# Relative attention on one core: scores that wait by pairs of heads, and three steps moved within a sequence's four quads

## The chip, the cores and the metric

The kernel runs on 1 core of one Trainium2 chip. The metric is the time of one execution in device microseconds (us), as the median of the runs shown. The program is a decoder of six stages in a row; the change touches one of them, the relative attention, and nothing before or behind it.

## What is computed

The stage takes 32 sequences of 100 rows (queries) of width 256 and, for each, a context of 361 rows (keys and values). It is attention with 16 heads of 16 channels, with a learnt vector for the distance between query and key in the scores, and another in the sum:

```python
rq, rk, rv = heads(query @ Wq + bq), heads(key @ Wk + bk), heads(value @ Wv + bv)
attn1 = einsum('bhqd,bhkd->bhqk', rq, rk)
attn2 = einsum('bhqd,qkd->bhqk', rq, rel_k_table[idx])
attn  = softmax((attn1 + attn2) / sqrt(16), axis=-1)
w1 = einsum('bhqk,bhkd->bhqd', attn, rv)
w2 = einsum('bhqk,qkd->bhqd', attn, rel_v_table[idx])
x = (w1 + w2).transpose(0, 2, 1, 3).reshape(b, t, 256) @ Wo + bo
```

`idx` is the distance from query to key, cut off at -32 and 32, plus 32. The stage's result is then x = layernorm(x + this). All of it is in 32-bit floats.

## The kernel before

**One turn per sequence, four quads in a turn.** `relative_cross` (L1827) runs a loop of turns, one for each of the 32 sequences, with each engine's instructions written out in a fixed order. The 16 heads go in four quads (`g` = 0 to 3) of four heads. The scores of a quad have the four banks of `rel_ps_s` in PSUM, one per head, and there is one set of them: a quad's scores may be written only when the weights of the quad before have been read out.

**A quad on three engines.** On TensorE, `scores` (L2334) computes four heads, each on 32 rows of the array of its own; the semaphore `s_s` is raised after the second and after the fourth. On VectorE, `maxima` (L2226) takes the heads in two pairs: it adds the distances' part (`rel_r_key`, L2235) and takes the negated maximum of each row (L2238). On ScalarE, `weights` (L2126) takes the exponentials of a pair (L2136), two instructions of one head each, and after the second pair raises `s_p`. Then ScalarE sends the quad's weights to DRAM (`store`, L2148).

**The transposes are one quad behind.** `weightsT` on TensorE transposes the weights of the quad before in three steps (c = 0, 1, 2, L2356) into the one bank `rel_ps_t`; after each, ScalarE copies it away (L2124) before the next may be written. `sums` on TensorE multiplies the values with the transposed weights of two quads before (`rel_ps_o`). So in quad g ScalarE's order is: copy 0, exponentials of pair 0, copy 1, exponentials of pair 1, copy 2.

**The jobs.** All else that TensorE does goes through the two banks of `rel_ps_m`, as 14 jobs per turn in the order of the table `JOBS`; a job's bank is its number modulo 2, and it may begin only when the job two before it, in the same bank, has been emptied by VectorE or ScalarE. `PLACES` has 16 places, four in each quad (place 4g behind the scores, 4g+1, 4g+2 and 4g+3 behind the transposes 0, 1 and 2), and says which jobs stand there. The jobs are `xT` and `q` (rows transposed, queries), `r0` and `r1` (the queries against the distance table, for the sequence two ahead), `k0`, `k1`, `v0`, `v1`, `v2` (keys and values of the next sequence), and of the sequence before: `den` (denominators; VectorE inverts them at L2216), `d0` and `d1` (transposes of the weights by distance, L2313), `w2` (sum with the distance table, L2321 and L2325) and `out` (output product).

**The weights by distance.** SyncE reads the stored weights of the sequence before back from DRAM by diagonals into `rel_by_dist`. Its first column, for all keys beyond the cut-off, is the far sum: GpSimd masks the weights (`rel_far`) and VectorE sums them at L2265, when both `rel_far` and the transfer are there. `d0` and `d1` wait for this sum. `den` waits for `rel_raw`, VectorE's copy of the finished sums of the sequence before (L2257), which waits for the last `sums` of that sequence; this stands on TensorE in quad 1, behind `r0`.

The loop of VectorE before, for each quad (L2250 and on): both pairs' maxima, in quad 1 the copy to `rel_raw`, then the jobs that VectorE empties, and at the end of quad 1 the far sum.

Of the kernel before, what the change touches and what calls it, by code (L numbers as in the profile page):

```python
# [12 lines left out]
AX = mybir.AxisListType  # L13
# [1813 lines left out]
def relative_cross(nc, io, keep):  # L1827
# [31 lines left out]
    with ExitStack() as ctx:  # L1859
# [55 lines left out]
        s_rpad = sem("distances_padded")  # L1915
        s_rout, s_rkey = sem("distances_in_dram"), [sem(f"distances_by_key{v}") for v in range(2)]
        s_s, s_add, s_neg, s_p = sem("scores"), sem("scores_added"), sem("maxima_negated"), sem("weights_ready")
        s_t, s_t_sb, s_pv, s_att = sem("weights_transposed"), sem("weightsT_stored"), sem("values_summed"), sem("sums_kept")
        s_pout, s_pdist, s_far, s_far_sum = ([sem(f"weights{v}_in_dram") for v in range(2)], sem("weights_by_distance"), sem("far_masked"),
                                             sem("far_summed"))  # L1920
# [3 lines left out]
        def head_of(g, j):  # L1924
# [2 lines left out]

        AHEAD = {"after": 2, "next": 1, "last": -1}
        JOBS = [("after", "xT"), ("next", "k0"), ("after", "q"), ("next", "k1"), ("after", "r0"), ("next", "v0"),
                ("after", "r1"), ("next", "v1"), ("last", "den"), ("last", "d0"), ("last", "d1"), ("last", "w2"),  # L1930
                ("next", "v2"), ("last", "out")]
        PLACES = [[0], [1], [2], [3], [4], [5], [6], [], [7], [8], [9, 10], [], [11], [12], [13], []]
        NUMBER = {what: n for n, (_, what) in enumerate(JOBS)}

        def bank(what):
# [151 lines left out]
        def _(act):  # L2087
            act.wait_ge(s_ready, 1)
            act.sem_inc(s_p, 1)

            def empty(t, place):
                for n, what, b in jobs(t, place):
# [33 lines left out]
            def weights(t, g, k):  # L2126
                if not t.within(B):
                    return
                act.wait_ge(s_neg, PAIRS * t.i + (2 * g + k + 1))
                if g == 0 and k == 0 and (not isinstance(t.i, int) or t.i > 1):  # L2130

                    act.wait_ge(s_pout[t.parity], 16 * GROUPS * t.half)
                    act.wait_ge(s_far, t.i - 1)
                for j in range(2 * k, 2 * k + 2):
                    slot = QUAD * g + j
                    last = nc.scalar.activation(prob[:, t.parity, slot, :], ps_s[0:S, j, 0:L], ACT.Exp,  # L2136
                                                bias=nmx[:, slot:slot + 1])
                if k == 1:
                    last.then_inc(s_p, 1)

            def store(b, g):
                if not b.within(B):
# [25 lines left out]
        def _(dve):  # L2168
# [79 lines left out]
            def turn(t):  # L2248
# [2 lines left out]
                    normalise(t + 2)  # L2251
                for g in range(GROUPS):
                    maxima(t, g, 0)
                    maxima(t, g, 1)
                    if g == 1 and prev.within(B):
                        dve.wait_ge(s_pv, GROUPS * prev.i + GROUPS)
                        nc.vector.tensor_copy(raw[:], ps_raw).then_inc(s_att, 1)  # L2257
                    for k in range(4):
                        if g == GROUPS - 1 and k == 2:
                            normalise(t + 3)  # L2260
                        empty(t, 4 * g + k)
                    if g == 1 and prev.within(B):
                        dve.wait_ge(s_far, prev.i + 1)
                        dve.wait_ge(s_pdist, 16 * prev.i + 16)
                        nc.vector.reduce_sum(by_dist[:, :, 0], far[:], AX.X).then_inc(s_far_sum, 1)  # L2265

            turns(dve, turn, -2, 3, B - 3, B + 1)

# [1 line left out]
        def _(pe):  # L2270
# [63 lines left out]
            def scores(t, g):  # L2334
                if not t.within(B):
                    return
                pe.wait_ge(s_p, GROUPS * t.i + (g + 1))
                if g == 0:
                    pe.wait_ge(s_qh, t.i + 1)
                    wait_emptied(pe, t + -1, "k1")  # L2340
                for j in range(QUAD):
                    rows = slice(j * TILE, (j + 1) * TILE)
                    last = mm(ps_s[0:S, j, 0:L], q_par[rows, t.parity, g % 2, g // 2, :], kT[rows, t.parity, g // 2, :], 0, 1)
                    if j % 2:
                        last.then_inc(s_s, 1)
# [621 lines left out]
```

## Time and profile before

| | |
|---|---|
| median of 3 runs | 2735.41 us |
| lowest and highest | 2733.01 and 2735.6 us |
| profiled execution, its own time | 2738.86 us |
| its span in the trace | 2737.1 us |
| granted clock of TensorE, mean of the span | 0.921 of full |
| TensorE (PE) busy in the span | 2340.4 us, 86% |
| VectorE (DVE) | 1495.7 us, 55% |
| ScalarE (ACT) | 1247.6 us, 46% |
| GpSimd (POOL) | 629.3 us, 23% |
| relative attention, first scores to last | 1452.0 to 2293.4 us |

The profile is of one execution; its own time stands 3.45 us above the median, and 1.76 us of it lie outside the span. The busy time of an engine is a share over all stages; the change has to be read from the relative attention alone, and there from one turn, since the turns repeat.

### The profile page before, as it was taken

Reading aid. Unit: us, or ns where it says so; the run is one execution under the profiler, and the core shown is the slowest. Engines: PE = TensorE matmul, PEld = TensorE weight load, DVE = VectorE, ACT = ScalarE, POOL = GpSimd, SP = SyncE. Lnnn points to the kernel's source line nnn. Section 1 sums busy time; section 2 is a strip of 40 time slices with the busy share of each in tenths; the row PEclk is TensorE's granted clock in tenths of the full one; section 3 lists DMA queues with packets and bytes.
Section 4 is the critical chain, followed back from the end, with each engine's and each line's share of the span. In section 5 each row is a group of like instructions: output and inputs, shape, how many; then the busy total and the mean of one; then the engine's idle time right before and its main releaser. Section 6 shows DMA issues by size and latency. Waiting matters only on the chain. (4 is left out here: it accounts for less than half of the span.)

```text
span 2737.1 us, 52948 instructions
## 1 busy us (share of the span) xinstructions
PE 2340.4 (86%) x18240; PEld 1860.6 (68%) x18240; DVE 1495.7 (55%) x2887; ACT 1247.6 (46%) x2737; POOL 629.3 (23%) x690
## 2 busy tenths in 40 slices
PE   8989999877999999489948999999999997695047
PEld 5669999767999999478835666666666665353035
DVE  5766666574111111268844666565666664644865
ACT  2223323211434343168734656555555654436753
POOL 1101111155434444534431121111121110000000
PEclk9999999968999999789968999999999997798579
DMA  2122322082999999500025555555455551110111
GB/s 81 53 72 70 78 71 65 22 281 81 341 342 345 341 348 342 174 1 0 0 45 135 128 125 125 128 122 122 119 128 125 125 125 48 59 57 0 50 46 42
DMA packets 375990, 339.40 MB, mean 124 GB/s; under 512 B 70227, under 2 KB 351853, under 8 KB 374637
## 3 DMA queue, kind: packets, MB, share of 16 engines
q1 hardware_dynamic: 311148, 294.82, 36.5%
q10 hardware_dynamic: 52480, 26.83, 3.9%
q0 software_dynamic: 12288, 16.79, 2.8%
q8 instruction: 44, 0.72, 0.1%
q14 instruction: 30, 0.24, 0.0%
HBM read 255.03 MB, written 83.37 MB: 124 GB/s over the span
## 5 line engine op out<-in xcount | busy, mean ns | idle before, releaser
L2124 ACT COPY rel_probT<-rel_ps_t 121x400 f32<-121x400 f32 x384 | 196.4, 511 | 259.5 <-PE rel_ps_t L2356 259.5
L2136 ACT ACTIVATE rel_prob<-rel_ps_s,rel_nmx 100x361 f32<-100x361 f32 x512 | 264.9, 580 | 2.1 <-DVE rel_nmx L2238 2.1
L2356 PEld LDWEIGHTS rel_ps_t<-rel_ident,rel_prob 100*121 100x121 f32 x1536 | 197.7, 187 | 78.1 <-ACT rel_probT L2124 49.2
L2356 PE MATMUL rel_ps_t<-rel_ident,rel_prob 100*121 100x100 f32 x1536 | 244.5, 282 | 7.2 <-ACT rel_probT L2124 7.2
L1328 PEld LDWEIGHTS moe_ps_h<-moe_xeT,moe_w 128*128 128x128 f32 x2048 | 241.3, 194 | 5.1 <-issue 1.9
L1328 PE MATMUL moe_ps_h<-moe_xeT,moe_w 128*128 128x128 f32 x2048 | 241.9, 277 | 1.3 <-DVE moe_xeT L1493 1.3
L2238 DVE TENSOR_REDUCE rel_nmx<-rel_ps_s 100x2 f32<-100x722 f32 x256 | 232.8, 909 | 8.8
L1328 PE MATMUL moe_ps_y<-moe_w,moe_hT 128*128 128x256 f32 x1024 | 231.4, 379 | 0.0
L1319 ACT ACTIVATE moe_hT<-moe_ps_h,moe_b 128x128 f32<-128x128 f32 x512 | 143.0, 375 | 138.4 <-PE moe_ps_h L1328 138.0
L2876 PE MATMUL ffd_ps_y<-ffn_w_dT,ffd_oq 128*100 128x256 f32 x384 | 85.9, 385 | 140.2 <-DVE ffd_oq L2821 134.6
L1328 PEld LDWEIGHTS moe_ps_y<-moe_w,moe_hT 128*128 128x128 f32 x1024 | 189.6, 190 | 23.2
L2235 DVE TENSOR_TENSOR rel_ps_s<-rel_ps_s,rel_r_key 100x262 f32<-100x262 f32 x256 | 110.9, 433 | 161.2 <-PE rel_ps_s L2272 159.4
L2876 PEld LDWEIGHTS ffd_ps_y<-ffn_w_dT,ffd_oq 128*100 128x100 f32 x384 | 64.6, 170 | 161.7 <-DVE ffd_oq L2821 135.2
L2063 POOL TENSOR_TENSOR rel_far<-rel_prob,rel_beyond 100x1088 f32<-100x1088 f32 x32 | 73.9, 2309 | 385.4 <-ACT rel_prob L2136 385.4
L1273 POOL DMA_INDIRECT moe_y_rows<-moe_ye,moe_place_out x64 | 102.6, 1603 | 196.4 <-DVE moe_ye L1509 187.2
L1504 DVE TENSOR_TENSOR moe_yb<-moe_ps_y,moe_b 128x256 f32<-128x256 f32 x64 | 27.2, 425 | 199.8 <-PE moe_ps_y L1328 199.8
L2652 PE MATMUL ffp_ps_h<-ffp_xqT,ffn_w_inT 128*128 128x400 f32 x384 | 132.9, 507 | 0.6 <-ACT ffp_xqT L2600 0.6
L2272 PE MATMUL rel_ps_s<-rel_kT,rel_q_par 32*100 32x361 f32 x1024 | 114.1, 515 | 20.7 <-ACT rel_prob L2136 20.7
L1620 POOL TENSOR_TENSOR cau_low<-cau_sc,cau_mx 100x800 f32<-100x800 f32 x64 | 101.6, 1593 | 118.8 <-DVE cau_mx L1702 118.7
L1493 DVE COPY moe_xeT<-moe_ps_T 128x256 f32<-128x256 f32 x64 | 27.2, 425 | 182.7 <-PE moe_ps_T L1380 179.9
L2076 POOL COPY rel_r_ext<-rel_r_ext 100x1072 f32<-100x1072 f32 x32 | 34.8, 1087 | 348.9 <-ACT rel_r_ext L2105 348.9
L2652 PEld LDWEIGHTS ffp_ps_h<-ffp_xqT,ffn_w_inT 128*128 128x128 f32 x384 | 73.4, 193 | 55.8 <-issue 2.3
(430 smaller groups left out, 4946.2 us busy)
## 6 DMA issues: line engine op xcount, KB each, us to landing
moe_w<-in_L_ffn_w SPq DMA_DIRECT2D x128, 1024.0 KB
rel_scores<-rel_r_ext SPq DMA_DIRECT2D x32, 818.8 KB
rel_r_key<-rel_scores SPq DMA_DIRECT2D x32, 818.8 KB
rel_weights<-rel_prob ACTq DMA_DIRECT2D x128, 204.7 KB
rel_by_dist<-rel_weights SPq DMA_DIRECT2D x32, 400.0 KB
mut_ctx_nat<-in_ctx SPq DMA_DIRECT2D x32, 363.0 KB
mut_ctx_T<-in_ctxT SPq DMA_DIRECT2D x16, 722.0 KB
rel_ctx_T<-in_ctxT SPq DMA_DIRECT2D x32, 361.0 KB, 3.3
```

The lines of the kernel that those rows point to most:

```text
L1273: nc.gpsimd.indirect_dma_start(out=y_rows[v][:], out_offset=bass.IndirectOffsetOnAxis(ap=place_out[:, v:v + 1], axis=0), in_=ye[:, v, :], ...
L1319: last = nc.scalar.activation(hT[:, v, k, :], ps_h[:, v, h, c * CAP:(c + 1) * CAP], ACT.Gelu, bias=at(b1, t.i)[:, k:k + 1])
L1328: return nc.tensor.matmul(out, lhsT, rhs, start=(k == 0), stop=(k == n - 1))
L1620: nc.gpsimd.tensor_tensor(low[:, half], sc[:, half], mx[:, half].unsqueeze(2).to_broadcast([S, HALF, S]), ALU.subtract).then_inc(s_low, 1)
L2124: nc.scalar.copy(probT[:, pg % 2, c], ps_pT).then_inc(s_t_sb, 1)
L2136: last = nc.scalar.activation(prob[:, t.parity, slot, :], ps_s[0:S, j, 0:L], ACT.Exp, bias=nmx[:, slot:slot + 1])
L2235: nc.vector.tensor_tensor(bank[:, :, 0:NEAR], bank[:, :, 0:NEAR], r_key[:, t.parity, two, :], ALU.add).then_inc(s_add, 1)
L2238: nc.vector.tensor_reduce(nmx[:, two], bank[:, :, 0:L], AX.X, ALU.max, negate=True).then_inc(s_neg, 1)
L2272: return nc.tensor.matmul(out, lhsT, rhs, start=(k == 0), stop=(k == n - 1))
L2356: last = nc.tensor.transpose(ps_pT[:, j, :], prob[:, pt.parity, QUAD * pg + j, c * STEP:c * STEP + R], ident[0:S, 0:S])
L2652: last = nc.tensor.matmul(ps_h[:, n % 4, 0:N], w_inT[:, k, j, c * P:(c + 1) * P], xqT[:, t.parity, j, :], start=(j == 0), stop=(j == KC - 1))
L2876: last = nc.tensor.matmul(ps_y[0:S, q, 0:D], oq[:, t.parity, c, q * S:(q + 1) * S], w_dT[:, c, :], start=(c == 0), stop=(c == IC - 1))
```

## The change

It has four parts. (1) ScalarE raises a new semaphore, `s_half`, after the exponentials of the first pair, and TensorE's first two heads of the next quad wait for that alone; the third and fourth wait for `s_p` as before. (2) `den` moves in the table from place 9 (quad 2, behind transpose 1) to place 6 (quad 1, behind transpose 1), `r1` from place 6 to 7, and `v1` from place 8 (behind the scores of quad 2) to place 9. (3) `d1` moves from place 10, where it stood right behind `d0`, to place 11, behind transpose 2. (4) On VectorE, the copy to `rel_raw` now stands between the two pairs' maxima of quad 1 and no longer behind them, and the far sum between those of quad 2 and no longer at the end of quad 1.

```diff
--- before.py
+++ after.py
@@ -1915,6 +1915,7 @@
         s_rpad = sem("distances_padded")
         s_rout, s_rkey = sem("distances_in_dram"), [sem(f"distances_by_key{v}") for v in range(2)]
         s_s, s_add, s_neg, s_p = sem("scores"), sem("scores_added"), sem("maxima_negated"), sem("weights_ready")
+        s_half = sem("first_half_weights")
         s_t, s_t_sb, s_pv, s_att = sem("weights_transposed"), sem("weightsT_stored"), sem("values_summed"), sem("sums_kept")
         s_pout, s_pdist, s_far, s_far_sum = ([sem(f"weights{v}_in_dram") for v in range(2)], sem("weights_by_distance"), sem("far_masked"),
                                              sem("far_summed"))
@@ -1927,9 +1928,9 @@
 
         AHEAD = {"after": 2, "next": 1, "last": -1}
         JOBS = [("after", "xT"), ("next", "k0"), ("after", "q"), ("next", "k1"), ("after", "r0"), ("next", "v0"),
-                ("after", "r1"), ("next", "v1"), ("last", "den"), ("last", "d0"), ("last", "d1"), ("last", "w2"),
+                ("last", "den"), ("after", "r1"), ("next", "v1"), ("last", "d0"), ("last", "d1"), ("last", "w2"),
                 ("next", "v2"), ("last", "out")]
-        PLACES = [[0], [1], [2], [3], [4], [5], [6], [], [7], [8], [9, 10], [], [11], [12], [13], []]
+        PLACES = [[0], [1], [2], [3], [4], [5], [6], [7], [], [8], [9], [10], [11], [12], [13], []]
         NUMBER = {what: n for n, (_, what) in enumerate(JOBS)}
 
         def bank(what):
@@ -2087,6 +2088,7 @@
         def _(act):
             act.wait_ge(s_ready, 1)
             act.sem_inc(s_p, 1)
+            act.sem_inc(s_half, 1)
 
             def empty(t, place):
                 for n, what, b in jobs(t, place):
@@ -2135,8 +2137,7 @@
                     slot = QUAD * g + j
                     last = nc.scalar.activation(prob[:, t.parity, slot, :], ps_s[0:S, j, 0:L], ACT.Exp,
                                                 bias=nmx[:, slot:slot + 1])
-                if k == 1:
-                    last.then_inc(s_p, 1)
+                last.then_inc(s_p if k else s_half, 1)
 
             def store(b, g):
                 if not b.within(B):
@@ -2251,18 +2252,18 @@
                     normalise(t + 2)
                 for g in range(GROUPS):
                     maxima(t, g, 0)
-                    maxima(t, g, 1)
                     if g == 1 and prev.within(B):
                         dve.wait_ge(s_pv, GROUPS * prev.i + GROUPS)
                         nc.vector.tensor_copy(raw[:], ps_raw).then_inc(s_att, 1)
+                    if g == 2 and prev.within(B):
+                        dve.wait_ge(s_far, prev.i + 1)
+                        dve.wait_ge(s_pdist, 16 * prev.i + 16)
+                        nc.vector.reduce_sum(by_dist[:, :, 0], far[:], AX.X).then_inc(s_far_sum, 1)
+                    maxima(t, g, 1)
                     for k in range(4):
                         if g == GROUPS - 1 and k == 2:
                             normalise(t + 3)
                         empty(t, 4 * g + k)
-                    if g == 1 and prev.within(B):
-                        dve.wait_ge(s_far, prev.i + 1)
-                        dve.wait_ge(s_pdist, 16 * prev.i + 16)
-                        nc.vector.reduce_sum(by_dist[:, :, 0], far[:], AX.X).then_inc(s_far_sum, 1)
 
             turns(dve, turn, -2, 3, B - 3, B + 1)
 
@@ -2334,12 +2335,14 @@
             def scores(t, g):
                 if not t.within(B):
                     return
-                pe.wait_ge(s_p, GROUPS * t.i + (g + 1))
+                pe.wait_ge(s_half, GROUPS * t.i + (g + 1))
                 if g == 0:
                     pe.wait_ge(s_qh, t.i + 1)
                     wait_emptied(pe, t + -1, "k1")
                 for j in range(QUAD):
                     rows = slice(j * TILE, (j + 1) * TILE)
+                    if j == 2:
+                        pe.wait_ge(s_p, GROUPS * t.i + (g + 1))
                     last = mm(ps_s[0:S, j, 0:L], q_par[rows, t.parity, g % 2, g // 2, :], kT[rows, t.parity, g // 2, :], 0, 1)
                     if j % 2:
                         last.then_inc(s_s, 1)
```

TensorE in the second quad, from `v0` (`rel_Wv`) to the scores of the third, before; `rel_ps_t` is a transpose step, `rel_tabT_heads` is `r1`:

```order
L2272 MATMUL rel_ps_m<-rel_Wv,rel_ctx_T 121x256 x2
L2354 REGISTER_ALU
L2356 MATMUL rel_ps_t<-rel_ident,rel_prob 121x100 x4
L2283 REGISTER_ALU
L2272 MATMUL rel_ps_m<-rel_tabT_heads,rel_qT 100x512
L2354 REGISTER_ALU
L2356 MATMUL rel_ps_t<-rel_ident,rel_prob 121x100 x4
L2337 REGISTER_ALU
L2272 MATMUL rel_ps_s<-rel_kT,rel_q_par 100x361 x4
```

The same stretch in the changed kernel (`rel_swap` is `den`):

```order
L2273 MATMUL rel_ps_m<-rel_Wv,rel_ctx_T 121x256 x2
L2357 REGISTER_ALU
L2359 MATMUL rel_ps_t<-rel_ident,rel_prob 121x100 x4
L2284 REGISTER_ALU
L2273 MATMUL rel_ps_m<-rel_raw,rel_swap 128x200 x2
L2357 REGISTER_ALU
L2359 MATMUL rel_ps_t<-rel_ident,rel_prob 121x100 x4
L2284 REGISTER_ALU
L2273 MATMUL rel_ps_m<-rel_tabT_heads,rel_qT 100x512
L2338 REGISTER_ALU
L2273 MATMUL rel_ps_s<-rel_kT,rel_q_par 100x361 x4
```

`den` has come in, and `r1` now stands right ahead of the scores.

TensorE in the third quad, from `den` to the scores of the fourth, before (`rel_by_dist` is `d0`, then `d1`):

```order
L2272 MATMUL rel_ps_m<-rel_raw,rel_swap 128x200 x2
L2354 REGISTER_ALU
L2356 MATMUL rel_ps_t<-rel_ident,rel_prob 121x100 x4
L2283 REGISTER_ALU
L2313 MATMUL rel_ps_m<-rel_ident,rel_by_dist 128x100 x4
L2283 REGISTER_ALU
L2313 MATMUL rel_ps_m<-rel_ident,rel_by_dist 128x100 x4
L2354 REGISTER_ALU
L2356 MATMUL rel_ps_t<-rel_ident,rel_prob 121x100 x4
L2337 REGISTER_ALU
L2272 MATMUL rel_ps_s<-rel_kT,rel_q_par 100x361 x4
```

The same stretch in the changed kernel:

```order
L2273 MATMUL rel_ps_m<-rel_Wv,rel_ctx_T 121x256 x2
L2357 REGISTER_ALU
L2359 MATMUL rel_ps_t<-rel_ident,rel_prob 121x100 x4
L2314 MATMUL rel_ps_m<-rel_ident,rel_by_dist 128x100 x4
L2357 REGISTER_ALU
L2359 MATMUL rel_ps_t<-rel_ident,rel_prob 121x100 x4
L2284 REGISTER_ALU
L2314 MATMUL rel_ps_m<-rel_ident,rel_by_dist 128x100 x4
L2338 REGISTER_ALU
L2273 MATMUL rel_ps_s<-rel_kT,rel_q_par 100x361 x4
```

`v1` stands where `den` stood, and `d1` is the last thing ahead of the scores.

VectorE in the changed kernel, third quad, from the maxima of the first pair to the emptying of `v1`:

```order
L2236 TENSOR_TENSOR rel_ps_s<-rel_ps_s,rel_r_key 100x2x131
L2239 TENSOR_REDUCE rel_nmx<-rel_ps_s 100x2
L2260 ISA
L2261 TENSOR_REDUCE rel_by_dist<-rel_far 100x16
L2235 REGISTER_ALU
L2236 TENSOR_TENSOR rel_ps_s<-rel_ps_s,rel_r_key 100x2x131
L2239 TENSOR_REDUCE rel_nmx<-rel_ps_s 100x2
L1959 REGISTER_ALU
L2214 TENSOR_TENSOR rel_vals<-rel_ps_m,rel_v_bias 121x8x2x16
```

The far sum has come between the two pairs; before, it stood ahead of both, and the two pairs' four instructions followed one another.

## Rows read from the trace of the kernel before

**Rows 1.** Windows: length, busy PE, PEld, DVE, ACT, POOL, then clock, DMA share, GB/s.

```profile
1920.00:2270.00 350.00, 330.11 (x3149) 229.92 (x3148) 218.98 (x358) 205.19 (x461) 63.04 (x52) 1.00 0.51 123
```

**Rows 2.** Waits of TensorE, then of VectorE, 1500 to 2300 us: total, times, longest.

```profile
PE rel_ps_m L2313 <- DVE rel_rec L2216: 20.0, 30, 0.8
...
DVE rel_by_dist L2265 <- DMA rel_by_dist<-rel_weights: 35.5, 29, 2.0
```

**Rows 3.** Timeline of TensorE, one turn: start, duration, instruction, [idle before it <- releaser].

```profile
2018.84 0.87 PE L2272 MATMUL rel_ps_s<-rel_kT,rel_q_par 32*100 32x361 f32 x8
2019.64 1.10 PE L2272 MATMUL rel_ps_m<-rel_tabT_heads,rel_qT 128*100 128x512 f32 x2
2020.67 0.72 PE L2272 MATMUL rel_ps_o<-rel_probT,rel_vals 120*32 120x100 f32 x24
...
2023.15 1.02 PE L2272 MATMUL rel_ps_m<-rel_tabT_heads,rel_qT 128*100 128x512 f32 x2
2024.01 0.60 PE L2356 MATMUL rel_ps_t<-rel_ident,rel_prob 100*121 100x100 f32 x4
2024.86 0.87 PE L2272 MATMUL rel_ps_s<-rel_kT,rel_q_par 32*100 32x361 f32 x8 [0.25 <-ACT rel_prob L2136]
...
2027.87 0.87 PE L2272 MATMUL rel_ps_m<-rel_raw,rel_swap 128*128 128x200 f32 x4
2028.61 0.67 PE L2356 MATMUL rel_ps_t<-rel_ident,rel_prob 100*121 100x100 f32 x4
2029.12 0.51 PE L2313 MATMUL rel_ps_m<-rel_ident,rel_by_dist 100*128 100x100 f32 x4
2030.24 0.56 PE L2313 MATMUL rel_ps_m<-rel_ident,rel_by_dist 100*128 100x100 f32 x4 [0.61 <-DVE rel_rec L2216]
2030.63 0.59 PE L2356 MATMUL rel_ps_t<-rel_ident,rel_prob 100*121 100x100 f32 x4
2031.15 0.87 PE L2272 MATMUL rel_ps_s<-rel_kT,rel_q_par 32*100 32x361 f32 x8
...
2038.55 0.87 PE L2272 MATMUL rel_ps_s<-rel_kT,rel_q_par 32*100 32x361 f32 x8 [0.44 <-ACT rel_prob L2136]
```

**Rows 4.** The source line of the scores in 2024.9:2025.0, then in 2025.5:2025.6: durations, first start.

```profile
L2272 PE MATMUL rel_ps_s<-rel_kT,rel_q_par x4: 542/542/542, 2024.9 to 2024.9; 32*100 32x361 f32 x4
L2272 PE MATMUL rel_ps_s<-rel_kT,rel_q_par x4: 462/462/462, 2025.2 to 2025.3; 32*100 32x361 f32 x4
```

**Rows 5.** Timeline of VectorE in the same turn; the last two are of the next.

```profile
2022.33 0.57 DVE L2257 COPY rel_raw<-rel_ps_o 128x400 f32<-128x400 f32 x1
...
2025.76 0.44 DVE L2235 TENSOR_TENSOR rel_ps_s<-rel_ps_s,rel_r_key 100x262 f32<-100x262 f32 x1 [0.21 <-PE rel_ps_s L2272]
2026.23 0.91 DVE L2238 TENSOR_REDUCE rel_nmx<-rel_ps_s 100x2 f32<-100x722 f32 x1
2027.06 0.43 DVE L2235 TENSOR_TENSOR rel_ps_s<-rel_ps_s,rel_r_key 100x262 f32<-100x262 f32 x1
...
2050.91 1.29 DVE L2265 TENSOR_REDUCE rel_by_dist<-rel_far 100x16 f32<-100x1088 f32 x1 [1.17 <-DMA rel_by_dist<-rel_weights]
2052.11 0.43 DVE L2235 TENSOR_TENSOR rel_ps_s<-rel_ps_s,rel_r_key 100x262 f32<-100x262 f32 x1
```

**Rows 6.** Timeline of ScalarE, same turn: exponentials of the second pair, in quads 1 and 3.

```profile
2023.76 1.05 ACT L2136 ACTIVATE rel_prob<-rel_ps_s,rel_nmx 100x361 f32<-100x361 f32 x2
...
2037.27 1.05 ACT L2136 ACTIVATE rel_prob<-rel_ps_s,rel_nmx 100x361 f32<-100x361 f32 x2
```

**Rows 7.** A disturbed turn: two windows, columns as in rows 1; TensorE's scores of quads 3 and 0.

```profile
1893.90:1897.30 3.40, 2.26 (x20) 1.79 (x24) 2.16 (x3) 2.98 (x8) 0.00 (x0) 1.00 0.68 163
1897.30:1900.70 3.40, 3.40 (x15) 2.40 (x8) 2.25 (x4) 0.33 (x1) 0.00 (x0) 0.50 0.47 109
...
1897.03 1.34 PE L2272 MATMUL rel_ps_s<-rel_kT,rel_q_par 32*100 32x361 f32 x8
1906.07 0.87 PE L2272 MATMUL rel_ps_s<-rel_kT,rel_q_par 32*100 32x361 f32 x8 [0.44 <-ACT rel_prob L2136]
```

## Prediction

> **What bounds the kernel now.** I read the windows first, then the waits, then the timeline of one turn on three engines. By the windows TensorE is busy for 330.11 of 350 us at the full clock (1.00, that is 2.4 GHz), while VectorE and ScalarE are at 219 and 205 us [rows 1]. So TensorE's own sequence sets a turn, and there are only two ways to win: less work on TensorE, or less waiting by it. The change removes no instruction of TensorE. What can be won is its waiting, and the timeline shows all of it in three places of a turn [rows 3]. Quad 1 (scores at 2018.84) ends at 2024.86: the last transposes begin at 2024.01, such a step ahead of scores takes 0.52 us where nothing holds it (2030.63 to 2031.15), so TensorE was ready at 2024.53 and waited 0.33 us for the exponentials. In quad 2, `d1` begins 1.12 us behind `d0` and itself takes 0.39 (2030.24 to 2030.63), so it waited 0.73 us, for VectorE's inverse of `den` that sits in its bank; this comes in every turn, 30 times for 20.0 us of idle engine [rows 2]. Quad 3 ends with an idle 0.44 us ahead of the scores at 2038.55. The quads last 6.02, 6.29 and 7.40 us.
>
> **Part 1, two semaphores for the scores.** TensorE may start the first pair of heads when the first two exponentials are done. What matters is what this is worth to the work behind. The four heads run side by side on their own rows: four of the eight records begin together at 2024.9, the other four, the second pass of each head, from 2025.2 on [rows 4], and the next instruction of the full array comes 0.80 us behind the first (2018.84 to 2019.64) [rows 3]. A head's two passes stand 0.38 us apart whether two or four heads run. So a pair that is issued late costs its own 0.80 us from its own start, and the early pair has saved nothing: what follows the scores still begins 0.80 us behind `s_p`. I price the overlap at **zero** on TensorE; the first pair's early scores only let VectorE begin sooner, and in quads 0, 1 and 3 ScalarE stands in its order behind the copy of the transposes, not behind the maxima. One small thing is won: at the end of quad 3 the scores come at 2038.55 though the exponentials ended at 2037.27 + 1.05 = 2038.32 [rows 6], 0.23 us, against 0.05 us in quad 1 (2023.76 + 1.05 = 2024.81, scores 2024.86), since quad 0's scores have two more waits to take in turn. These will now be taken ahead of the first pair. **-0.18 us** per turn, between 0 and -0.23.
>
> **Part 2, `den` in quad 1.** It takes 0.74 us of TensorE (2027.87 to 2028.61) [rows 3]. In quad 1 it meets a stall of 0.33, which it fills. Besides, `r1` now stands right ahead of the scores; `r0` ahead of the sums takes 1.03 us, `r1` ahead of a transpose 0.86, so a change of array shape costs it 0.17. Quad 1, ready after 2024.53 - 2018.84 = 5.69 us, becomes 5.69 + 0.74 + 0.17 = 6.60 us, against 6.02: **+0.58 us**. The bounds are 0.41 (no cost of the shape) and 0.75. The Trainium skill (TensorEngine Tiling (Array Packing), Key Properties) says that a change of tiling mode drains the engine. By it the move also takes one such change away, since `v1` no longer stands between the scores and the sums of quad 2, so the stage has as many as before; this sum would not change, as quad 2 will be bound by something else.
>
> **Part 4 in quad 1, the copy to `rel_raw` ahead of the second pair.** It waits for the sums, which begin at 2020.67 and take 0.72: copy from about 2021.45, 0.57 us long [rows 5], so the second pair's add starts at about 2022.05 and its maxima end 0.47 + 0.91 us later, at 2023.45. The exponentials of that pair began at 2023.76, held by ScalarE's copies. Cost **zero**; the cover is 0.3 us, and without it each tenth of a us goes to `s_p`, which TensorE now needs only at 6.60, 0.6 us later than before. `den` itself stands where `r1` stood, at 2023.15, 1.1 us behind the end of the copy.
>
> **Parts 3 and 4 in quad 2.** The wait of 0.73 us for the inverse goes: it will have been computed in quad 1. What is late next is the far sum. Count from the first scores of quad 2, which stand at 0. The add of the first pair starts at 0.90 (2024.86 to 2025.76), the next instruction of VectorE 1.30 later (to 2027.06), at 2.20 [rows 5]. There stands the far sum now, whose follower starts 1.20 us behind it (2050.91 to 2052.11): 3.40. Then add 0.47, maxima 0.91: 4.78. Then 0.05 for the semaphore, 1.05 for the two exponentials, 0.05 again: the second pair of quad 3's scores starts at **5.93**, and all work behind it 0.80 later. TensorE's own work in the quad is less, 6.29 - 0.73 - 0.74 = 4.82. `d1` has a new wait too, as its bank is now that of `v1`, which VectorE empties behind the second pair's maxima, at about 4.70 + 0.43 (as an add) = 5.15; with 0.39 for `d1` the first pair could start at 5.6. Both waits lie side by side and the later one, 5.93, decides. Quad 2: **-0.36 us** against 6.29. Bounds: -1.47 (4.82, the far sum hidden) and 0 (every step of the chain with 0.04 more).
>
> **Late transfers.** VectorE waits for the weights by distance 29 times, 35.5 us in all, 1.22 on average and 2.0 at most, where the turn shown has 1.17 [rows 2, 5]. The far sum is now asked for some 3 us later in the turn, so what came late will be there: 29 x 0.05 = **-1.6 us** in all.
>
> **The sum.** Per turn -0.18 + 0.58 - 0.36 = +0.04 us; over 30 turns +1.2 us, less 1.6: -0.4 us. From the profiled execution's 2738.86 that is 2738.5; the median of the runs stands 3.45 lower, at 2735.41, and gives 2735.0. What is won at one wait is paid at another: the far sum takes the place of the inverse.
>
> **Rivals.** *The far sum stays hidden* (faster). If the second pair's exponentials of quad 2 were not held by VectorE, that quad would fall to the larger of TensorE's own 4.82 us and the chain without the far sum, 5.93 - 1.20 = 4.73; I take 5.1, to leave room for ScalarE's copies between the pairs, another 0.83 us in 30 turns, -25 us: **2710**. For it speaks that VectorE is idle for over a third of the stretch [rows 1]. Against it, its instructions stand in order, and each link above has its row.
>
> *The pairs don't overlap* (slower). Where both semaphores are long up, in quads 1 and 2, the wait that now stands between the pairs may keep the second from starting beside the first; it would start at the earliest with the first pair's second pass, 0.38 us later [rows 4]. That is 0.38 us in quad 1 and up to as much in quad 2 (0.3 of it covered by the chain), 0.38 to 0.76, I take 0.5: 30 x 0.5 = +15 us, **2750**. No row has a wait between heads on different rows of the array, so rows neither show nor exclude it. It decides as soon as an upheld semaphore delays the third head by over 0.1 us. The Trainium skill (TensorE: Matmul & The Clock Gate, The mechanism) says that matmuls start and end in program order, without reordering. By that rule a head's second pass would stand ahead of the next head, and the second pair would start behind it, this case exactly; the rows disagree, since four records begin together and the second passes 0.38 us behind them, so I give the case less than the rule would.
>
> *The clock* (slower). In one turn a late far sum left TensorE busy for only 2.26 of 3.40 us; then the clock stood at 0.50, that is 1.2 GHz, and the quad behind lasted 9.04 us where 7.40 is usual [rows 7]: 1.64 us. The change brings the waits of quad 2 together ahead of quad 3's scores (some 1.1 us in 5.93), and half the array runs in the first pair. If a third of the turns drop, that is +16 us, **2751**; if all do, +49 us.
>
> **Chances.** Forecast 0.66; the far sum hidden 0.10; no overlap 0.15; the clock 0.09. The forecast's own range is 2728 to 2742: its three terms may each be off by 0.1 us, 0.2 together, 6 us in 30 turns. What a measurement of this kernel can tell from no change is 0.2%, 5.5 us, so 2729.9 and 2740.9 are the borders. Of the forecast I put 0.18 below them, 0.42 between and 0.06 above. With the rivals: faster 0.18 + 0.10 = 0.28, same 0.42, slower 0.06 + 0.15 + 0.09 = 0.30. The range of 2725 to 2752 leaves out the far sum hidden and the clock in more than a third of the turns, with small ends of the forecast.
>
> **What would show it.** In the changed profile: quad 1 of 6.6 us with no wait at its end; the inverse gone from the waits of TensorE; `d1` waiting for `rel_vals`; the second pair of quad 3's scores some 5.9 us behind quad 2's, with the exponentials as releaser; VectorE's far sum with no wait for its transfer. I am wrong if quad 2 comes out at 5.1 (the far sum is hidden), if the third head starts 0.38 us behind the first with `s_p` long up, or if the granted clock of the stretch falls below 1.00.

## The result and the profile after

The changed kernel takes **2723.66 us** (median of 5 runs, 2718.51 to 2726.74) against 2735.41 (2731.53 to 2737.12, 5 runs) of the kernel before on the same chip: a ratio of **0.9958, 95% interval 0.9945 to 0.9972**. It is faster by 0.42%, outside the 0.2% that I had called no change, and 1.3 us below the low end of my range. On a second chip (run s6 below) it stood against the kernel before at 0.9982 (0.9970 to 0.9993), 4.9 us under it where the first chip has 11.75, so the size of the gain is less certain than one interval says; it lies between some 5 and 12 us. The profiled execution has an own time of 2724.02 us, a span of 2722.3 and a mean granted clock of 0.926.

The windows of the changed kernel: first turn, second turn, then 750 us of like turns (columns as in [rows 1]):

```profile
1450.37:1472.16 21.79, 18.15 (x151) 11.68 (x151) 12.98 (x23) 12.96 (x29) 2.72 (x4) 1.00 0.68 165
1472.16:1498.25 26.09, 25.38 (x239) 17.95 (x239) 15.94 (x26) 15.78 (x36) 4.89 (x4) 1.00 0.58 133
...
1500.00:2250.00 750.00, 728.75 (x6810) 510.35 (x6798) 472.12 (x771) 451.29 (x1002) 138.87 (x114) 1.00 0.52 125
```

The same three of the kernel before:

```profile
1451.98:1478.78 26.80, 21.53 (x152) 13.79 (x151) 13.45 (x23) 13.24 (x29) 3.55 (x6) 0.85 0.67 153
1478.78:1507.24 28.46, 27.36 (x239) 18.83 (x239) 16.32 (x27) 15.85 (x36) 4.76 (x4) 0.90 0.48 111
...
1500.00:2250.00 750.00, 711.72 (x6742) 493.90 (x6743) 465.58 (x764) 440.52 (x990) 137.94 (x113) 1.00 0.52 125
```

In the like turns TensorE is now busy for 97% where it was 95%. But the first turn became shorter by 5 us and the second by more than 2, and in both the clock of before is below full where that of after is 1.00.

Waits of the changed kernel in 1500 to 2290 us (total, times, longest), those of TensorE on the changed jobs:

```profile
PE rel_ps_m L2314 <- DVE rel_vals L2214: 13.7, 28, 0.5
PE rel_ps_m L2314 <- DVE rel_by_dist L2261: 6.2, 28, 0.2
PE rel_ps_t L2359 <- ACT rel_probT L2126: 5.4, 10, 0.7
```

The inverse of [rows 2] is gone, as is VectorE's wait for the transfer by distance: no row of its waits has `rel_by_dist` any more. The `d` jobs wait for the far sum and for `rel_vals`, 20 us in all, as much as for the inverse before. One turn on TensorE (columns as in [rows 3]):

```profile
2004.01 0.87 PE L2273 MATMUL rel_ps_s<-rel_kT,rel_q_par 32*100 32x361 f32 x8
...
2008.32 0.86 PE L2273 MATMUL rel_ps_m<-rel_raw,rel_swap 128*128 128x200 f32 x4
2009.11 0.67 PE L2359 MATMUL rel_ps_t<-rel_ident,rel_prob 100*121 100x100 f32 x4
2009.62 1.02 PE L2273 MATMUL rel_ps_m<-rel_tabT_heads,rel_qT 128*100 128x512 f32 x2
2010.57 0.87 PE L2273 MATMUL rel_ps_s<-rel_kT,rel_q_par 32*100 32x361 f32 x8
...
2014.20 0.53 PE L2314 MATMUL rel_ps_m<-rel_ident,rel_by_dist 100*128 100x100 f32 x4 [0.22 <-DVE rel_by_dist L2261]
2014.57 0.67 PE L2359 MATMUL rel_ps_t<-rel_ident,rel_prob 100*121 100x100 f32 x4
2015.72 0.56 PE L2314 MATMUL rel_ps_m<-rel_ident,rel_by_dist 100*128 100x100 f32 x4 [0.49 <-DVE rel_vals L2214]
2016.22 1.07 PE L2273 MATMUL rel_ps_s<-rel_kT,rel_q_par 32*100 32x361 f32 x8
...
2023.32 1.18 PE L2273 MATMUL rel_ps_s<-rel_kT,rel_q_par 32*100 32x361 f32 x8
2024.42 0.39 PE L2289 MATMUL rel_ps_m<-rel_ident,rel_xn 100*128 100x100 f32 x2
```

Quad 1 (2004.01 to 2010.57) lasts 6.56 us and has no wait at its end. Quad 2's cause stands on VectorE in the same turn:

```profile
2011.47 0.44 DVE L2236 TENSOR_TENSOR rel_ps_s<-rel_ps_s,rel_r_key 100x262 f32<-100x262 f32 x1 [0.84 <-PE rel_ps_s L2273]
2011.94 0.91 DVE L2239 TENSOR_REDUCE rel_nmx<-rel_ps_s 100x2 f32<-100x722 f32 x1
2012.77 1.28 DVE L2261 TENSOR_REDUCE rel_by_dist<-rel_far 100x16 f32<-100x1088 f32 x1
2013.96 0.43 DVE L2236 TENSOR_TENSOR rel_ps_s<-rel_ps_s,rel_r_key 100x262 f32<-100x262 f32 x1
2014.43 0.91 DVE L2239 TENSOR_REDUCE rel_nmx<-rel_ps_s 100x2 f32<-100x722 f32 x1
```

and on ScalarE:

```profile
2015.37 1.01 ACT L2138 ACTIVATE rel_prob<-rel_ps_s,rel_nmx 100x361 f32<-100x361 f32 x2 [0.85 <-DVE rel_nmx L2239]
```

ScalarE sits idle for 0.85 us until the maxima behind the far sum are there; its exponentials end at 2016.38, and the second pair of scores follows at 2016.4.

**Where the time went.** Lengths by the starts of the second pair of scores, in us, from two profiled executions of each kernel (the second ones are runs s11 and s6 below; of turns 3 to 28 the usual turn stands in brackets):

| | before | before, again | after | after, again |
|---|---|---|---|---|
| turn 0 | 26.80 | 24.49 | 22.10 | 21.44 |
| turns 1 and 2 | 54.93 | 53.18 | 52.16 | 52.15 |
| turns 3 to 28 | 689.24 (26.39) | 685.30 (26.38) | 682.79 (26.26) | 682.76 (26.26) |
| turns 29 and 30 | 51.83 | 50.76 | 50.04 | 50.03 |

The usual turn gives 26 x 0.13 = 3.4 us. Everything else in these turns, 4 us by the second columns and 12 by the first, comes from the start of the stage, from its end, and from turns of before that were disturbed. Outside these turns executions differ too: the turns of the second pair are 7.4 us apart, their spans only 3.5.

### The profile page after: what moved, and what is told of

Read it like the earlier page. It is cut to its first block and busy times, and to the rows that moved or that the text cites. A ratio compares the mean times of both kernels' runs of the same rounds, so it can differ in the third digit from the quotient of the medians.

```text
span 2722.3 us, 52898 instructions
## 1 busy us (share of the span) xinstructions
PE 2345.8 (86%) x18240; PEld 1870.3 (69%) x18240; DVE 1496.6 (55%) x2887; ACT 1252.7 (46%) x2737; POOL 628.5 (23%) x690
## 5 line engine op out<-in xcount | busy, mean ns | idle before, releaser
L2138 ACT ACTIVATE rel_prob<-rel_ps_s,rel_nmx 100x361 f32<-100x361 f32 x512 | 263.9, 576 | 27.0 <-DVE rel_nmx L2239 26.8
L2273 PE MATMUL rel_ps_s<-rel_kT,rel_q_par 32*100 32x361 f32 x1024 | 127.5, 505 | 0.4
```

The costliest lines, as they stand in the source:

```text
L2273: return nc.tensor.matmul(out, lhsT, rhs, start=(k == 0), stop=(k == n - 1))
```

## The experiments

The usual turn of each kernel with its four quads, medians of turns 3 to 28 in us, is the measure that tells the parts apart; the ratio is that of the whole times:

| kernel | quad 0 | 1 | 2 | 3 | turn | ratio to before (95%) |
|---|---|---|---|---|---|---|
| before (s11) | 6.64 | 6.02 | 6.29 | 7.40 | 26.38 | |
| after (s6) | 6.65 | 6.56 | 5.85 | 7.20 | 26.26 | 0.9982 (0.9970 to 0.9993) |
| s1, pairs only | 6.65 | 6.01 | 6.29 | 7.20 | 26.19 | 0.9997 (0.9986 to 1.0007) |
| s3, after without pairs | 6.65 | 6.56 | 5.86 | 7.40 | 26.47 | 0.9982 (0.9972 to 0.9993) |
| s2, table only | 6.64 | 6.56 | 4.93 | 7.40 | 25.55 | 0.9889 (0.9873 to 0.9905) |
| s4, after, far sum back | 6.65 | 6.56 | 4.94 | 7.20 | 25.38 | 0.9890 (0.9874 to 0.9906) |
| s7, after, raw copy back | 6.65 | 6.56 | 5.85 | 7.20 | 26.26 | one run |
| s12, after, `d1` at `d0` | 6.65 | 6.56 | 6.07 | 7.20 | 26.48 | 1.0041 (1.0024 to 1.0058) |
| s9, before, `v1` moved | 6.65 | 6.02 | 6.19 | 7.40 | 26.29 | 0.9977 (0.9968 to 0.9987) |
| s10, s4 with `v1` ahead | 6.65 | 6.56 | 5.99 | 7.20 | 26.43 | one run |
| s5, s4 with `w2` later | 6.64 | 6.56 | 4.93 | 6.92 | 25.06 | 0.9856 (0.9840 to 0.9873) |

**s1 and s3: the pairs alone, and all but the pairs.** s1 puts this edit alone into the kernel before, s3 takes it out of the changed one:

```diff
-                if k == 1:
-                    last.then_inc(s_p, 1)
+                last.then_inc(s_p if k else s_half, 1)
...
-                pe.wait_ge(s_p, GROUPS * t.i + (g + 1))
+                pe.wait_ge(s_half, GROUPS * t.i + (g + 1))
...
+                    if j == 2:
+                        pe.wait_ge(s_p, GROUPS * t.i + (g + 1))
```

> The kernel before with part 1 alone (the two semaphores for the scores). Theory A (only the waits ahead of quad 0's scores are shortened, what stands behind the scores is bound by the second pair): the usual turn falls from 26.39 to about 26.21 us, some 5 us in all, about 2730 us. Theory B (the split is what made the change faster, since VectorE gets each first pair sooner): the usual turn falls by 0.4 us or more, 2724 us or less.

> The changed kernel without part 1. Theory A: the usual turn rises from 26.26 to about 26.44 us, 5 us in all, 2729 us. Theory B (the split carries the gain): at least 10 us more than the changed kernel, 2734 us or more.

s1: 2731.71 us beside 2733.26 of the kernel before, the same; s3: 2729.58. In both directions the edit moves one quad and no other: quad 3 is 7.20 with it and 7.40 without. That is 0.20 us per turn, the semaphores that are taken early. ScalarE's last exponentials of quad 3 in the changed kernel:

```profile
2022.54 1.05 ACT L2138 ACTIVATE rel_prob<-rel_ps_s,rel_nmx 100x361 f32<-100x361 f32 x2
```

They end at 2023.59, and the second pair of scores starts at 2023.64, 0.05 us later, where it was 0.23 before.

The time of s1 doesn't show the gain. In its one profile the first turn lasted 29.20 us, with two stretches at a clock of 0.50 in it, against 24.5 and 26.8 in the two profiles of the kernel before, and its turns 0 to 30 come to 814.5 us beside 822.8 and 813.7. Whether the first turn took the gain from the median too isn't shown. So a part's worth in the like turns and the time of the whole are two things here.

**s2 and s4: the far sum back at the end of quad 1.** s2 is the kernel before with the new `JOBS` and `PLACES` and nothing else; s4 is the changed kernel with

```diff
-                    if g == 2 and prev.within(B):
-                        dve.wait_ge(s_far, prev.i + 1)
-                        dve.wait_ge(s_pdist, 16 * prev.i + 16)
-                        nc.vector.reduce_sum(by_dist[:, :, 0], far[:], AX.X).then_inc(s_far_sum, 1)
                     maxima(t, g, 1)
                     for k in range(4):
...
                         empty(t, 4 * g + k)
+                    if g == 1 and prev.within(B):
+                        dve.wait_ge(s_far, prev.i + 1)
+                        dve.wait_ge(s_pdist, 16 * prev.i + 16)
+                        nc.vector.reduce_sum(by_dist[:, :, 0], far[:], AX.X).then_inc(s_far_sum, 1)
```

> The kernel before with the new table of jobs alone (den in quad 1, d1 apart from d0), the far sum still at the end of quad 1, no split. Theory A (the far sum between the maxima took back most of what the moved den freed): quad 1 lasts about 6.6 us, quad 2 only 5.1, the usual turn is 25.8 us, the time about 2717 us or less, faster than the whole change. Rival (the far sum's place is free, the moved den itself is worth little): turn 26.3 us or more, 2728 to 2735 us.

> The changed kernel with the far sum back at the end of quad 1, all else as changed. Theory A (the chain through the far sum bounds quad 2): quad 2 falls from 5.87 to about 5.1 us, the usual turn to 25.5 us, the time to about 2700 us. Rival (quad 2 is bound by d1's wait for the emptied v1 or by the late transfer, which would now be waited for again): no gain, 2720 to 2728 us.

s2 takes 2703.9 us, s4 2702.6, beside 2733.26 of the kernel before: **of the 31 us that the rest of the change wins, the far sum's new place takes 21 to 23 back.** Quad 2 falls to 4.93, 0.92 less than in the changed kernel, and further than I had expected of s2 (5.1 us, and 2717 for the whole). In s2 TensorE's quad 2 is:

```profile
2023.67 0.87 PE L2272 MATMUL rel_ps_s<-rel_kT,rel_q_par 32*100 32x361 f32 x8
...
2027.66 0.67 PE L2356 MATMUL rel_ps_t<-rel_ident,rel_prob 100*121 100x100 f32 x4 [0.25 <-ACT rel_probT L2124]
...
2028.60 0.87 PE L2272 MATMUL rel_ps_s<-rel_kT,rel_q_par 32*100 32x361 f32 x8
```

All that is left of waiting is 0.25 us for ScalarE's copy. In its old place the far sum stands in time that VectorE has to spare: in s4 it delays the add behind it by some 0.2 us, and the quad isn't longer for it. VectorE in a usual turn of s4, at the end of quad 1 (scores of quad 2 at 2019.64):

```profile
2018.29 1.41 DVE L2217 RECIPROCAL rel_rec<-rel_ps_m 128x200 f32<-128x200 f32 x1 [0.39 <-PE rel_ps_m L2273]
2019.61 1.23 DVE L2266 TENSOR_REDUCE rel_by_dist<-rel_far 100x16 f32<-100x1088 f32 x1
2020.76 0.42 DVE L2236 TENSOR_TENSOR rel_ps_s<-rel_ps_s,rel_r_key 100x262 f32<-100x262 f32 x1
```

The wait for the transfer is gone too, though the far sum is where it was. From 1500 to 2230 us VectorE waits for it 27 times in the kernel before (32.7 us in all), twice in s4 (1.3 us) and never in s2. The inverse of `den` now stands ahead of the far sum in VectorE's order, so the sum is asked for later: this came with the table of jobs and needed no move of the far sum. Turns 3 to 28 of s4 come to 659.43 us, 23.4 less than in the changed kernel; its first turn was 2.2 longer; the spans differ by 21.2.

**s7: the copy to `rel_raw` back behind both maxima of quad 1,** in the changed kernel:

```diff
-                    if g == 1 and prev.within(B):
-                        dve.wait_ge(s_pv, GROUPS * prev.i + GROUPS)
-                        nc.vector.tensor_copy(raw[:], ps_raw).then_inc(s_att, 1)
...
                     maxima(t, g, 1)
+                    if g == 1 and prev.within(B):
+                        dve.wait_ge(s_pv, GROUPS * prev.i + GROUPS)
+                        nc.vector.tensor_copy(raw[:], ps_raw).then_inc(s_att, 1)
```

> The changed kernel with the copy to rel_raw behind both pairs' maxima of quad 1 again. My sum priced this part at zero: quad 1 stays at 6.56 us and the turn at 26.26 us, within 0.03. If the copy's place matters for den, den waits and quad 1 grows by over 0.1 us.

2725.21 us, with the changed kernel (s6) at 2725.27 on the same chip, and the same four quads. Turns 3 to 28 are 682.75 and 682.76 us. In the changed kernel this part is worth nothing.

**s6 and s11: both kernels once more.** The changed kernel is unaltered in s6, the kernel before in s11.

> The changed kernel once more, unaltered, for a common baseline with its neighbours. Usual turn 26.26 us, quad 2 to the second pair 5.85 us, 2723 us, 0.4% under the kernel before. If the gain of the first turn (22.1 us instead of 26.8) were a chance of the clock in one profile, it would be absent here in the trace.

> The kernel before, unaltered, for a second profile. If the half clock in its first two turns and the 26.8 us of the first are its own and no chance, they are here again: quads 2 and 3 of the first turn 5.9 us or more each and a stretch at 0.50 of the clock within its first 20 us of turns. The usual turn is 26.39 us, with some turns longer by 0.2 to 2 us.

s6: 2725.27 us (2719.31 to 2731.27, 12 runs) against 2730.16. s11: 2722.87 in its one run, beside a median of 2730.45 (2725.76 to 2738.66, 21 runs). Turn by turn the two profiles of the changed kernel agree to 0.03 us from turn 1 to 28. Those of the kernel before don't: they differ by 2.3 us in turn 0, 1.8 in turns 1 and 2, 3.9 in 3 to 28. s11's first two turns:

```profile
1447.70:1472.20 24.50, 19.84 (x151) 12.56 (x150) 13.44 (x23) 13.24 (x30) 3.45 (x5) 0.93 0.71 156
1472.20:1498.60 26.40, 25.11 (x238) 17.50 (x238) 16.04 (x27) 15.64 (x36) 4.89 (x4) 1.00 0.53 127
```

The clock of its first turn is 0.93 where the first profile has 0.85, and at full clock the second turn takes 26.40 us, not 28.46. So the half clock in the first turn came again, and the long second turn did not.

**s8 and s12: `d1` back beside `d0`,** one run, then ten:

```diff
-        PLACES = [[0], [1], [2], [3], [4], [5], [6], [7], [], [8], [9], [10], [11], [12], [13], []]
+        PLACES = [[0], [1], [2], [3], [4], [5], [6], [7], [], [8], [9, 10], [], [11], [12], [13], []]
```

> The changed kernel with d1 right behind d0 again. d1 must still wait for v1 to be emptied, now with transpose 2 behind it: the second pair of quad 3's scores would move from 5.85 to about 6.0 us behind quad 2's (d1 at 5.15, 0.4 for it, 0.45 for the transpose), the turn from 26.26 to 26.4 us. If the far sum's chain alone decides, the turn stays at 26.26.

> The changed kernel with d1 right behind d0 once more, now timed. If the ten drops of the clock in its turns were of that kernel (its waits of quad 2 come at one place, 0.2 us longer), they come again and it is about 20 us slower than the changed kernel, 2740 us or more. If they were a chance of one run, it is 6 us slower by the 0.21 us of quad 2 alone, about 2731 us.

s8: 2744.97 us; s12: 2742.26 (2734.82 to 2750.96, 10 runs), slower than the kernel before. The waits of s12, 1500 to 2200 us:

```profile
PE rel_ps_m L2314 <- DVE rel_vals L2214: 25.8, 26, 1.0
PE rel_ps_m L2314 <- DVE rel_by_dist L2261: 5.7, 26, 0.2
```

`d1` meets the same wait one transpose earlier, 1.0 us at once in place of 0.5, and quad 2 grows by 0.22 us. That explains a quarter of it. Turns 3 to 28 are 703.1 us in s8 and 704.7 in s12, 20.3 and 21.9 more than in the changed kernel, and the turns without a drop account for 26 x 0.21 = 5.5. The rest is the clock: s8 has nine short stretches at 0.50 in these turns and s12 ten, where the changed kernel has none, and each turn with one is 1.64 us longer than its like without (28.08 for 26.44, 28.15 for 26.51), 14.8 and 16.4 us in all. One of them with what came right before it (windows, as in [rows 7]):

```profile
1541.10:1544.50 3.40, 2.19 (x23) 1.60 (x22) 1.97 (x4) 2.55 (x8) 0.00 (x0) 1.00 0.61 153
1544.55:1547.95 3.40, 3.40 (x16) 2.80 (x9) 2.60 (x4) 0.45 (x2) 0.00 (x0) 0.50 0.66 147
```

TensorE was busy for 2.19 of 3.40 us ahead of the drop; [rows 7] had 2.26. So a step moved by one place is worth 20 us in the turns, three quarters of it by the clock.

**s9 and s10: `v1` behind transpose 0, alone and undone.** s9 makes this one move in the kernel before; s10 is s4 with `v1` back ahead of transpose 0:

```diff
-        PLACES = [[0], [1], [2], [3], [4], [5], [6], [], [7], [8], [9, 10], [], [11], [12], [13], []]
+        PLACES = [[0], [1], [2], [3], [4], [5], [6], [], [], [7, 8], [9, 10], [], [11], [12], [13], []]
```

> The kernel before with v1 alone moved from place 8 (ahead of the sums of quad 2) to place 9 (behind transpose 0); den, d0 and d1 stand where they stood. In the usual turn den's inverse still holds d1, so quad 2 stays at 6.2 to 6.3 us and the turn at 26.4. If v1's place is what shortens the first turn (ScalarE's copy 0 and all exponentials behind it come 1.05 us sooner there), quads 2 and 3 of the first turn are 4.9 us each instead of 5.97 and 7.92 and no drop of the clock follows them, and the time falls by about 5 us. If the first turn's gain comes from den's move, they stay near 6 us.

> The changed kernel with the far sum back at the end of quad 1 (2702.6 us, quad 2 4.93 us) and v1 back in place 8, ahead of the sums. If v1's place is half of what quad 2 won, ScalarE's chain is 1.05 us later, quad 2 is about 5.9 to 6.0 us and the turn about 26.4. If den's move alone gave it, quad 2 stays at 4.9 to 5.0 us, 25.4 for the turn.

s10: 2739.43 us in its one run, 37 more than s4 on another chip (31.7 in turns 3 to 28, some 5 of it by three turns with a drop of the clock, the shown one among them), and its quad 2 is 5.99 where s4's is 4.94. TensorE in s10, quad 2:

```profile
2019.78 0.87 PE L2273 MATMUL rel_ps_s<-rel_kT,rel_q_par 32*100 32x361 f32 x8
2020.58 1.12 PE L2273 MATMUL rel_ps_m<-rel_Wv,rel_ctx_T 128*121 128x256 f32 x4
...
2023.53 0.67 PE L2359 MATMUL rel_ps_t<-rel_ident,rel_prob 100*121 100x100 f32 x4 [0.58 <-ACT rel_probT L2126]
2024.83 0.67 PE L2359 MATMUL rel_ps_t<-rel_ident,rel_prob 100*121 100x100 f32 x4 [0.29 <-ACT rel_probT L2126]
```

`v1` (1.12 us) stands between the scores and transpose 0, and so ahead of ScalarE's first copy. ScalarE needs from that copy on 2.7 us for copy, exponentials, copy, exponentials, whatever TensorE does meanwhile; all of it begins 1.05 us sooner once `v1` is out of the way. In the usual turn of the kernel before little is won by that, since the inverse decides there: s9 has 6.19 for 6.29. In the first turn there are no jobs of a sequence before and nothing else decides. ScalarE in quad 2 of the first turn, before (scores at 1464.89):

```profile
1468.09 0.49 ACT L2124 COPY rel_probT<-rel_ps_t 121x400 f32<-121x400 f32 x1 [2.39 <-PE rel_ps_t L2356]
...
1469.76 1.05 ACT L2136 ACTIVATE rel_prob<-rel_ps_s,rel_nmx 100x361 f32<-100x361 f32 x2
```

and after (scores at 1462.67):

```profile
1464.82 0.49 ACT L2126 COPY rel_probT<-rel_ps_t 121x400 f32<-121x400 f32 x1 [1.46 <-PE rel_ps_t L2359]
...
1466.50 1.03 ACT L2138 ACTIVATE rel_prob<-rel_ps_s,rel_nmx 100x361 f32<-100x361 f32 x2
```

The copy comes 3.20 us behind the scores before and 2.15 after; the quad falls from 5.97 to 4.90. s9's first turn is 22.72 us, against 24.49 and 26.80, and s9 as a whole is at 0.9977: this one number of the table brings about as much as the whole change in s6. The moves also need each other. With `v1` left ahead (s10) the rest of the table takes only 0.30 us from quad 2 and puts 0.54 on quad 1, a loss; `v1` alone (s9) takes 0.10; both together (s2, s4) take 1.36.

The clock of the first turn goes with `v1`'s place. All four profiles of kernels that have `v1` ahead of transpose 0 (before, s11, s1, s10) fall to 0.50 some 19 to 21 us behind their first scores, two of them also 6 to 7 us behind; their first turns last 24.49 to 29.20 us. Of the ten that have it behind, none falls at 19 to 21 us, and one (s4) does at 6 us; their first turns last 21.44 to 22.72 us, s4's 24.29.

**s5: the same thing done for `w2`, with the far sum back.** `w2` stood in quad 3 where `v1` had stood in quad 2, right behind the scores:

```diff
-        PLACES = [[0], [1], [2], [3], [4], [5], [6], [7], [], [8], [9], [10], [11], [12], [13], []]
+        PLACES = [[0], [1], [2], [3], [4], [5], [6], [7], [], [8], [9], [10], [], [11, 12], [13], []]
```

> The changed kernel with the far sum back at the end of quad 1, and w2 moved from place 12 (ahead of transpose 0 of quad 3) to place 13 (ahead of v2). If the wait left at the end of quad 3 is ScalarE's order (exponentials behind the copy of transpose 0, which w2's 2.2 us hold back), the second pair of quad 0's scores no longer starts 0.31 us behind the first, the turn falls from 25.38 to about 25.1 us and the time to about 2694 us. If w2's own waits for d1's copy take its place, the turn stays at 25.4 us, about 2703 us.

2689.69 us (2685.31 to 2692.42), 0.9856 (0.9840 to 0.9873): 40 us under the kernel before and 36 under the changed one on that chip, the fastest kernel of this study. Quad 3 falls from 7.20 to 6.92; the other quads are those of s4. In one point the expectation failed: the second pair of quad 0's scores still starts 0.30 us behind the first in the usual turn.

## Why the prediction was wrong, point by point

**What failed is the line "the sum".** It ran over 30 like turns, +0.04 us each, and took 1.6 off for late transfers. Of the 11.75 us measured, the like turns give 3.4. Three things are missing from it or wrong in it. The miss is narrow: with the 2725.27 us of the second chip the time would have been just inside the range.

- *The first turn had no term.* There `den`, the inverse, `d0` and `d1` don't exist, so the bound that I wrote down for quad 2, the inverse, doesn't either. Behind it stood ScalarE, held up by `v1` (s9, s10). I had named `v1`'s move only for the changes of array shape. In turn 0 it is 1.07 us in quad 2; quad 3, 4.90 us now, had been 7.92 and 6.46, all of it at half clock in the first profile and part in the second. Quad 0 fell by 1.1 and 1.0 us, and there it isn't `v1`: TensorE's wait for `rel_xn` is 0.37 us at most in all ten profiles with the new table and 1.07 at least in the four with the old one, s9 among them. The changed kernel has two waits of 0.52 us just ahead of its first scores that the kernel before hasn't, so this part may only have crossed the border of the turn. The turn as a whole fell by 4.7 us in the first pair of profiles and 3.05 in the second.
- *The clock was priced in one direction.* I had it only as a rival that slows the changed kernel, and took from the one drop of the kernel before at 1897 [rows 7] no more than what a drop costs. The kernel before was at half clock for 13.65 us from 1470.6 in one profile, which also lengthened its second turn, and for 3.4 us from 1466.2 in the other; the changed kernel has no drop between its first scores and 2259 us in either. What it avoids so is part of the gain: quad 3 of turn 0 has the same steps in the same order in both kernels, and at full clock it takes 4.90 us, so the 3.0 and 1.6 us that it was longer are the clock's, and with them the 2.0 us by which the second turn of the first profile exceeds that of the second. The mechanism of the rival is real, one step away: s12 falls ten times in 26 turns.
- *The steady terms were 0.17 us per turn too high.* Pairs: -0.18 forecast, -0.20 measured (s1, s3). `den` in quad 1: +0.58, measured +0.54; the quad has no wait at its end, 6.56 us, with `den` at 0.79 us where I had 0.74 and `r1` ahead of the scores at 0.95 where I had 1.03. Quad 2: -0.36, measured -0.44, since the chain's last links were short: exponentials of 1.01 for 1.05 us, and hand-overs under 0.05. The three add up to -0.10, the turns themselves to -0.13, where I had +0.04: 26 x 0.17 = 4 us, inside the 6 that I had allowed.

The *late transfers* were right in kind: VectorE's wait is gone from the changed kernel. But it goes with the table of jobs alone (s2), so the far sum's new place wasn't what removed it. In size, what the kernel before spends beyond its usual turn in 3 to 28 is 689.24 - 26 x 26.39 = 3.1 us in one profile, 1.64 of it at the drop, and nothing in the other. So -1.6 holds for one execution and 0 for the next.

**What was right.** The far sum took the place of the inverse: quad 2 is ended by the exponentials behind it, and with it moved back (s4) the quad is 0.91 us shorter. `d1` waits for `rel_vals`. The copy to `rel_raw` costs nothing (s7). A pair that is issued late costs its own 0.80 us from its own start: at 2023.32 the first pair starts, 0.32 later the second, and `xT` comes at 2024.42, 0.78 behind the second.

**The rivals.** *Far sum hidden*: false in the changed kernel, but its estimate of 25 us was near what s4 then won (21 to 23). Its quad of 5.1 was 4.93. *The pairs don't overlap*: false. In quad 2 of the turn shown, the source line of the scores has in the first 0.05 us:

```profile
L2273 PE MATMUL rel_ps_s<-rel_kT,rel_q_par x4: 542/542/543, 2010.6 to 2010.6; 32*100 32x361 f32 x4
```

Four records in 0.02 us, the third head 0.013 us behind the first, with a wait between them that is long met. Where the second pair is late, at 2023.32, two records start and two follow:

```profile
L2273 PE MATMUL rel_ps_s<-rel_kT,rel_q_par x2: 542/542/542, 2023.3 to 2023.3; 32*100 32x361 f32 x2
...
L2273 PE MATMUL rel_ps_s<-rel_kT,rel_q_par x4: 542/542/542, 2023.3 to 2023.6; 32*100 32x361 f32 x4
```

The first pair's second passes start at 2023.70, behind the third head, which started at 2023.64. By the rule of program order (the Trainium skill, TensorE: Matmul & The Clock Gate, The mechanism), which says that matmuls start and end in the order of the program, a head's second pass would have had to come ahead of the third head. Taken pass by pass, these rows disagree with it for heads on different rows of the array, and the measurement decides. Taken head by head they keep it: the heads start in order, and their second passes in order too. The prediction had read the rule pass by pass.

**What stays open.** How much of the gain is the clock in the first turns can't be fixed: single executions of the kernel before lie between 2721 and 2740 us in these runs, and two profiles of it differ by 16.0 us in span, 4.3 of it ahead of the stage's first scores and 9.1 within turns 0 to 30. The changed kernel isn't free of drops at the stage's end either. That `v1`'s place brings the half clock of the first turn rests on 4 profiles against 10, and no run takes `v1` alone back in the changed kernel.

## What to carry to other kernels

Cost a pipelined loop's first and last turns by themselves: jobs are missing there, so another engine sets the pace, and a step that is covered in the steady turn is bare in them. When a moved step stands directly behind an engine's long job, ask which other engine's whole chain starts behind it; a job between the scores and the first transpose was worth 1.05 us here, more than the longest wait of TensorE in [rows 2]. And before work is moved into the gap between two halves of a stage, see whether those halves are what the next stage waits for: the far sum cost the quads nothing that they show at the end of quad 1, and 0.9 us between the maxima of quad 2.

## What the runs showed of the hardware that I had not expected

Where the waits stand together, TensorE's clock fell more often: with 1.0 us at once in quad 2 (s8, s12) there were nine and ten stretches at 0.50 in 26 turns, and with 0.5 and 0.2 us apart (the changed kernel, two profiles) none. Of the 20.3 and 21.9 us between them, 14.8 and 16.4 are what the drops added to their turns. A half-clock stretch at the same place can also differ in length from one execution to the next: in the first turn of the kernel before it lasted 13.7 us in one profile and 3.4 in the other, and that turn's last quad 7.92 and 6.46 us.
